# Weight pieces split one slot later, and loads handed out three stores ahead, in a deformable-convolution and normalisation kernel

## The reference

```python
# layer 0
out = relu(bn(conv1x1(x, w1)))                 # 1024 -> 256 channels
offset = conv3x3(out, w_off, b_off)            # 18 channels
out = relu(bn(deform_conv3x3(out, offset, w2)))
x1 = relu(bn(conv1x1(out, w3)) + x)            # 256 -> 1024
# layer 1, per image
t, p, g = Wt @ x1, Wp @ x1, Wg @ x1            # 512 channels each
# three sums over the image of (p^o * g), o = 0..2, give att
y = sum_o att[o] * alpha[o] * t ** o
z = Wz @ y                                     # 512 -> 1024
out = (z - mean(z)) * rsqrt(var(z) + eps) * gn_w + gn_b + x1
```

## Time and profile before

| | us |
|---|---|
| median of 3 runs | 2363.9 (2363.74 to 2366.23) |
| the profiled execution, its own time | 2355.59 |
| its span (first to last instruction) | 2353.8 |
| PE busy in it | 2243.0 (95%) |
| DVE, ACT, POOL busy | 1572.7, 1252.0, 778.6 |
| mean granted TensorE clock | 0.981 |

### The profile page before, as it was taken

The page is one execution under the profiler, slowest core; times in us unless marked ns, Lnnn a source line. Parts: engine busy times, 40 slices in busy tenths (PEclk is TensorE's granted clock), DMA queues, the critical chain, the costliest instruction groups (busy, mean ns, idle before and its releaser), DMA issues.

```text
span 2353.8 us, 29804 instructions
## 1 busy us (share of the span) xinstructions
PE 2243.0 (95%) x10252; PEld 1853.8 (79%) x10252; DVE 1572.7 (67%) x3177; ACT 1252.0 (53%) x2432; POOL 778.6 (33%) x706
## 2 busy tenths in 40 slices
PE   8999999999989999999999999999999999999970
PEld 6888888888868788888878888788788878887750
DVE  4212325766788898889878988789785324557855
ACT  6444444444465666556655665565553324446745
POOL 0100003333224565556556765666561000000000
PEclk9999999999989999999999999999999999999985
DMA  8988989999998998889889988898884111118979
GB/s 304 320 310 279 314 291 381 403 400 394 401 375 286 315 341 308 297 320 336 288 294 315 314 313 307 295 313 305 289 305 156 60 49 53 54 50 288 314 229 388
DMA packets 289824, 667.97 MB, mean 284 GB/s; under 512 B 27112, under 2 KB 101608, under 8 KB 283528
## 3 DMA queue, kind: packets, MB, share of 16 engines
q0 software_dynamic: 88048, 322.81, 39.4%
q1 hardware_dynamic: 172536, 262.59, 31.4%
q10 hardware_dynamic: 29088, 80.67, 9.4%
HBM read 435.47 MB, written 230.49 MB: 283 GB/s over the span
## 4 chain that ended last, share of the span: by engine, by line
PE 86%; DMA 5%; DVE 5%; SPq 1%; issue 1%; ACT 1%; POOL 0%; ACTq 0%; DVEq 0%
PE bank L194 22%; PE bank L196 22%; PE bank L195 22%; PE bank L1462 5%; PE bank L1463 5%; PE bank L1464 5%; DVE z L1406 2%; PE bank L1480 2%; DMA xs<-x 2%; DMA g<-vwide,tbl 1%; DMA out<-z 1%; PE bank L1488 1%; PE bank L1504 1%; DMA xt<-x 0%; DVE zst L1371 0%
## 5 line engine op out<-in xcount | busy, mean ns | idle before, releaser
L647 POOL DMA_INDIRECT g<-vwide,tbl x512 | 589.9, 1152 | 548.9 <-DVE a L1018 208.1
L194 PE MATMUL bank<-x1h,wlh 128*128 128x512 f32 x1536 | 604.2, 393 | 5.4 <-DVE x1l L1296 3.9
L196 PE MATMUL bank<-x1h,wll 128*128 128x512 f32 x1536 | 601.6, 392 | 2.5 <-issue 2.5
L195 PE MATMUL bank<-x1l,wlh 128*128 128x512 f32 x1536 | 600.6, 391 | 2.8 <-issue 2.7
L1034 DVE SCALAR_TENSOR_TENSOR a<-g,tbl,a 128x256 f32<-128x256 f32 x1224 | 528.8, 479 | 23.7 <-DMA g<-vwide,tbl 18.4
L674 ACT ACTIVATE g<-g,tbl 128x256 f32<-128x256 f32 x1008 | 426.4, 499 | 200.2 <-DMA g<-vwide,tbl 158.1
L194 PEld LDWEIGHTS bank<-x1h,wlh 128*128 128x128 f32 x1536 | 289.4, 188 | 66.5 <-issue 6.1
L196 PEld LDWEIGHTS bank<-x1h,wll 128*128 128x128 f32 x1536 | 289.1, 188 | 66.8 <-issue 4.6
L195 PEld LDWEIGHTS bank<-x1l,wlh 128*128 128x128 f32 x1536 | 289.6, 189 | 66.0 <-issue 5.4
L752 ACT ACTIVATE vb<-bank 128x512 f32<-128x512 f32 (+1 forms) x320 | 174.3, 554 | 195.3 <-PE bank L1464 150.7
L1462 PE MATMUL bank<-w2h,o1h 128*128 128x512 f32 (+1 forms) x640 | 236.7, 370 | 0.0
(11 more groups left out here) (154 smaller groups left out, 3204.1 us busy)
## 6 DMA issues: line engine op xcount, KB each, us to landing
vwide<-vb SPq DMA_DIRECT2D x256, 256.0 KB, 4.3
vwide<-vb SPq DMA_DIRECT2D x112, 512.0 KB, 4.2
xf<-in_x SPq DMA_DIRECT2D x32, 1024.0 KB
x<-xf ACTq DMA_DIRECT2D x32, 1024.0 KB, 6.8
out<-z SPq DMA_DIRECT2D x128, 256.0 KB, 5.2
xin<-in_x ACTq DMA_DIRECT2D x54, 512.0 KB
t<-ts ACTq DMA_DIRECT2D x64, 256.0 KB
tb<-t POOLq DMA_DIRECT2D x16, 1024.0 KB, 5.4
```

Of the source, the lines that this page charges most:

```text
L194: nc.tensor.matmul(out, wh, xh, start=first, stop=False)
L195: nc.tensor.matmul(out, wh, xl, start=False, stop=False)
L196: return nc.tensor.matmul(out, wl, xh, start=False, stop=last)
L647: pool.indirect_dma_start(slot[:].rearrange("p a c -> p (a c)"), None, d["vwide"][img], bass.IndirectOffsetOnAxis(ap=at[:, i, tap(u), 0:1] ...
```

## The change

Two edits. In chunk 0 of the second stage the pieces 5 to 13 are split in slots 1 to 9 in place of 0 to 8, on ACT and on DVE. In the last convolution SP's list is reordered: in both loops a load comes ahead of the store that is three places earlier than before, so that `load_xs(i + 4)`, which waits for `sum_done` of i + 1, stands in front of `store_out(i - 3)`, and `load_x1` of an odd i in front of `store_out(i - 3)`.

```diff
             for i in range(len(XS)):
                 load_xs(i)
-            for i in range(ZT):
+            for i in range(ZT + 3):
                 if i + len(XS) < ZT:
                     load_xs(i + len(XS))
-                store_out(i)
+                if i >= 3:
+                    store_out(i - 3)
...
-            for i in range(ZT, IMGS * ZT):
-                store_out(i)
+            for i in range(ZT, IMGS * ZT + 3):
+
                 j = i // 2 + len(XT)
                 if i % 2 and j < ZT:
                     load_x1(j)
+                if i >= ZT + 3:
+                    store_out(i - 3)
...
-                    if c == 0 and 5 + q < 2 + GROUPS:
-                        split_high(5 + q)
+                    if c == 0 and q and 4 + q < 2 + GROUPS:
+                        split_high(4 + q)
...
-                    if c == 0 and 5 + q < 2 + GROUPS:
-                        split_low(5 + q)
+                    if c == 0 and q and 4 + q < 2 + GROUPS:
+                        split_low(4 + q)
```

## The result

Five runs of each kernel on one chip: 2383.51 us with the change (2380.4 to 2394.88), 2363.9 without (2358.25 to 2366.85). The ratio is 1.0102, with a 95% interval of 1.0076 to 1.0127: slower by 1.0%, which is some 24 us (18 to 30). The profiled execution took 2382.32 us at a clock of 0.976, against 2355.59 at 0.981.

What follows compares the result with a forecast made beforehand. PE was taken as the bound (86% of the chain), DMA in the tail. First edit 0, chain 19.3, half clock 2.1, tail 0 gave +21.4 us on 2363.9, so 2385.3; 8-in-10 range 2375 to 2395.

Steps and rivals of the forecast that it cites:

- the chain that was written down: Last convolution, image 0: evictions 71 to 75 and 77 each wait for a store the one before releases; 19.3 us later.
- Start of the chain: Last convolution: store 0, in the same crowd as tb's 1 MB load, releases eviction 71 at 2128.1.
- The rule that the DMA engines take turns between queues: At store 0: it would not wait for all of tb's 1 MB; eviction 71 at some 2125.5, sum 2.6 us less.
- The step: Eviction to next eviction through add, load, store and landing: 5.24 us, or 6.08 with `y_square`; three and two of them.
- PE's waits: Last convolution: about 5 us before tile 78, about 10 before tile 80 for yl, then half clock costing 2.1 us.
- Gain at the later chunks: Last convolution: xs loads no longer wait behind `fin`, which could end PE's yl waits; taken 0, bound -3.8 us.
- The first edit: Chunk 0 of the second stage, later splits: 0 us in sum, from -3.4 to +3.1.
- the bad side of the weighing: Chunk 0: an early gather runs beside the last vb stores; 1 MB in front of them is 2.6 us.
- The gathers of unit 35: Chunk 0: unit 35 is summed some 6 us earlier, so its two gathers go at about 671 instead of 676.76.
- The new wait for `wll` at slot 3: Chunk 0: PE waits 2.0 us at slot 3 because piece 5 is split one slot later.
- PE's wait for o2l: Chunk 0: o2l ready at 701.2 as before, so PE's wait shrinks from 5.9 by 2.0 us, to some 4.
- The tail: End of the last convolution: DMA engines are full, so order inside the queue costs nothing; 0 us, bounds -1 and +1.

Runs made afterwards that it cites:

- the list of image 0 alone: Kernel before with only image 0's stores three places later, in the first loop of the last convolution: 2391.51 us, ratio 1.0108.
- three places from store 12 on: Kernel before with image 0's stores 0 to 11 unchanged and all its later ones three places late: 2352.38 us, ratio 0.9988.
- the splits and store 12: Kernel before with the nine pieces split one slot later and image 0's stores three places late from store 12 on: 2334.9 us, ratio 0.9981.
- the change with earlier adds: Changed kernel with image 0's adds started earlier, six instead of four made by tile 71's statistics: 2364.98 us, 0.9992 of the kernel before.
- image 1's list alone: Kernel before with only image 1's stores three places later, in the second loop (the tail): 2366.62 us, ratio 1.0001.
- the first place: Kernel before with image 0's stores one place later: 2350.34 us in one run, where the kernel before had 2354.2.
- the second: Kernel before with image 0's stores two places later: 2356.08 us in one run, where the kernel before had 2354.2.

## Why the prediction was right, and which terms were off

**The forecast and its cause.** 2385.3 was forecast, 2383.51 measured. That they are only 1.8 us apart is luck: five runs of the kernel after spread over 14 us. The mechanism was that of the prediction: the list of image 0 alone has the loss, adds moved ahead undo it, and the evictions 71, 72, 73, 74, 75 and 77 are the chain that was written down.

**Start of the chain.** Eviction 71 was taken at 2128.1, 10.0 us behind eviction 70; it came 10.24 behind. From add 3 it was 7.9 us, and is 8.17 (2126.59 to 2134.76). The rule that the DMA engines take turns between queues (the Trainium skill, DMA: Bandwidth & Descriptors, Queues, rings and completion order) would have given 5.3. The trace speaks against that use of it here, as in the earlier trace rows. Store 0, issued at 2127.71, took 7.0 us and landed after the 1 MB of tb, issued at 2125.94. DMA queues of the kernel after, 2129 to 2131 us (q0 carries tb, q1 is SP's):

```profile
q0 software_dynamic: 81, 0.66, 92.5%
q1 hardware_dynamic: 1, 0.00, 0.0%
```

Before, around store 2, both queues moved at once (2121 to 2125 us: 0.87 MB and 0.18), and that store took 7.6 us all the same. So turns or not, the store was no earlier; why SP's queue stood still after, no run shows.

**The step, mis-sized.** This is the term of the sum that was mis-sized most. Landing was taken as 2.6 us and measured 3.3: in this chain a load of 0.25 MB is always issued 0.37 us ahead of the store on the same queue. (That the load is the reason is argued; no run has the chain without it.) Load to store on SP was 0.36, not 0.53. The step from 2140.78 to 2146.51 is 1.24 to the add (2142.02), 0.76 to the load (2142.78), 0.36 to the store (2143.14), 3.28 to its landing and 0.09 to the eviction: 5.73. (The add's start is from the timeline; the chain starts each piece where the one before it ends.) The steps without `y_square` are 5.73 to 6.02 for 5.24, those with it 6.41 and 6.44 for 6.08, together 30.4 us for 27.9. The delay at tile 80 is 21.9 for 19.3.

**PE's waits.** Predicted were 5 and 10 us, with a half clock behind the second; they are 6.67 and 13.55. The eight products behind the second start 0.44 us apart, from 2168.61 to 2172.15, 3.54 us where 8 x 0.233 is 1.86: 1.7 us, for 2.1. That the clock also fell behind the first wait costs nothing, since PE waits again.

**Gain at the later chunks.** The prediction took 0 and named 3.8 as the bound. PE's waits for yl at the four later chunks, 3.2 us, are gone: this was inside the bound, but the term itself was wrong. They are gone too with three places from store 12 on, where nothing else is late, so the earlier loads do it. From tile 80 on the kernel gets 2.5 us back: 3.2, less the 1.7 of the clock, and 1.0 that is not explained.

**The first edit.** Taken as 0, from -3.4 to +3.1. It is a gain of 2 to 3 us in the time to the expansion, seen in four profiles against ten; the run of splits alone (0.9981, 0.9951 to 1.0011) can't tell it from none. The step that failed is the bad side of the weighing, 1 MB in front of the vb stores: they landed 2.3 us earlier, not later. The gathers of unit 35 did move up, by 3.2 us in place of 6. The new wait for `wll` at slot 3 was to be 2.0 us. It was none in the kernel after and with splits alone, 0.24 with the splits and store 12, and 1.97 in the change with earlier adds; timeline of PE there:

```profile
679.35 0.50 PE L194 MATMUL bank<-x1h,wlh 128*128 128x512 f32 x1 [1.97 <-DVE wll L1088]
```

In all four the split was ready some 19 us after slot 0's first product, and not 21.5, since it stands behind the vb stores. What differs is when PE comes to slot 3. Behind the wait for x1l 11 and 14 products start 0.43 us apart or more in the kernel after and with splits alone, and slot 3 begins at 19.3 and 19.8 us; with the earlier adds none does, and PE stands ready at 17.0. So this wait hangs on how many products run at the half clock there, and it cost nothing at the expansion, where PE waits anyway. PE's wait for o2l shrank to 3.8, as forecast (some 4).

**The tail.** Taken as 0, bounds -1 and +1. In the time it can't be told from nothing (image 1's list alone: 1.0001, 0.9979 to 1.0023), but the traces show a cost of 0.9 us. From the end of PE's last small product to the end of the span it is 70.8 to 71.2 us in the three profiles with image 1's list changed, and 69.7 to 70.3 in the eleven without. So "order inside a full queue costs nothing" doesn't quite hold here. Where the 0.9 us goes isn't shown: the first DMA goes out as early as before (2.7 us behind that product, 2.8 before), and in the first 10 us behind it 2.9 MB move after and 3.0 before.

**The sum.** Terms as measured in the profile: -2.1 + 21.9 - 2.5 + 0.9 = +18.2 us for the parts that the change touches, against the forecast +21.4; the medians differ by 19.6, and by the ratio the loss is 24 (18 to 30). The forecast was near because errors of both signs were in it: a chain 2.6 too short and a tail 0.9 too short, and gains of 2.1 us in the first edit and 4.2 behind tile 80 (-2.5 with the 1.7 of the clock, forecast as 2.1, taken off) that were taken as nothing.

## What to carry to other kernels

Where a buffer is reused, follow one place around: who frees it, what the freeing stands behind in its queue, and what that waits for. If the way comes back to the reuse itself, a tile takes the latency of the loop divided by the tiles that fit in it, or the time of the busiest engine where that is more. So the first place costs little (20.7 us from eviction 70 to 77, for 18.5 without), the second some 8 us (27.1), because the loop then leaves no time to make up one late store, and the third very much (40.6). Loads may well be handed out ahead of stores, but only from the point where the stores' release runs ahead of their need (here from store 12).

## What the runs showed of the hardware that was not expected

- A DMA issue on POOL isn't of fixed length: the same gather took 0.94 us beside an idle DVE, and 4.38 where it began in the midst of 16 sums of DVE with two inputs each from SBUF. The Trainium skill (GPSIMD Engine Reference, Specifications) says that GpSimd's way to SBUF is shared with VectorE and contended when DVE has two SBUF inputs. The traces agree: in all 14 profiles every gather issued wholly beside an idle DVE took 0.93 to 0.98 us. Those issued wholly beside DVE's two-input work took 1.08 to 1.09 in the median and up to 2.6, so such work doesn't by itself make an issue long; what does isn't shown.
- A store of 0.25 MB lands in 3.3 us when a load of the same size is issued 0.37 us ahead on its queue; the median of three stores in a quiet stretch with a load between them was 2.6, and the shortest 2.0.
- With stores landing one at a time the DMA engines moved 137 GB/s at a share of 0.41, against 240 at 0.73 in the same work before.
